# Local attention, layer norm and a routed feed-forward layer on one core: GpSimd splits a tile's attention ahead of the row's norm

## The reference

```python
qkv = x @ W_attn + b_attn                      # 16 heads of 16
scores = einsum(q, k) * scale                  # causal, 64 rows back
out = softmax(scores) @ v
x = layernorm(x + out @ W_proj + b_proj)       # eps 1e-5
# routed feed-forward: argmax of 8 router logits picks the expert
inter = gelu(x @ W1[e] + b1[e])                # 256 -> 1024
y = inter @ Wo + bo + x
y = (y - mean(y)) * rsqrt(var(y) + 1e-12) * gamma + beta
x = layernorm(y)
```

## Time and profile before

| | |
|---|---|
| time, median of 3 runs | 637.53 us (636.71 to 638.04) |
| time of the profiled execution | 635.29 us |
| its span | 633.6 us |
| granted TensorE clock, mean | 0.916 of full |
| PE busy | 83% of the span |
| DVE, ACT, POOL busy | 63%, 58%, 51% |

### The profile page before, as it was taken

How to read it: one execution, slowest core, us unless ns; L and a number is a source line. 1 busy time by engine, 2 the same in 40 slices (tenths; PEclk the granted TensorE clock), 3 DMA queues, 4 the chain that set the end, 5 groups by cost and what they waited for, 6 DMA issues and landing times. The chain is left out here.

```text
span 633.6 us, 24795 instructions
## 1 busy us (share of the span) xinstructions
PE 523.3 (83%) x8587; PEld 456.2 (72%) x8587; DVE 397.6 (63%) x1071; ACT 370.0 (58%) x832; POOL 325.9 (51%) x568
## 2 busy tenths in 40 slices
PE   4698878788878878788787761799999999999990
PEld 3487667677766767667675660699999999999880
DVE  3445546575565657565674446578888888887533
ACT  4357466675656566667564632476667666765450
POOL 8612333533442353344533433168888888887333
PEclk9779799996998999999995765799999999999996
DMA  9787597465645655665464200223322222222000
GB/s 207 166 219 209 154 228 197 127 176 129 178 134 136 186 149 157 152 178 175 134 156 137 64 12 24 68 62 101 96 87 78 77 78 70 77 66 66 24 16 6
DMA packets 94888, 75.34 MB, mean 119 GB/s; under 512 B 37030, under 2 KB 88367, under 8 KB 94770
## 3 DMA queue, kind: packets, MB, share of 16 engines
q1 hardware_dynamic: 91410, 65.31, 39.8%
q0 software_dynamic: 3264, 8.41, 3.8%
q10 hardware_dynamic: 96, 0.04, 0.0%
HBM read 43.63 MB, written 23.62 MB: 106 GB/s over the span
## 5 line engine op out<-in xcount | busy, mean ns | idle before, releaser
L1409 PE MATMUL ps<-v_even,w_hi 128*128 128x128 f16 (+1 forms) x1280 | 170.3, 215 | 1.9 <-issue 0.8
L1409 PE MATMUL ps<-v_even,w_lo 128*128 128x128 f16 (+1 forms) x640 | 132.0, 214 | 0.2
L835 ACT ACTIVATE probs<-ps,b1T 128x128 f32<-128x128 f32 (+1 forms) x320 | 87.3, 361 | 72.2 <-PE ps L1409 63.7
L1391 PE MATMUL ps<-wo_hi,ks 128*128 128x256 f16 x576 | 128.6, 272 | 1.0 <-DVE ks L1084 1.0
L1409 PEld LDWEIGHTS ps<-v_even,w_hi 128*128 x1280 | 120.7, 98 | 7.0 <-issue 3.6
L868 DVE TENSOR_REDUCE mx<-ps 128x4 bf16<-128x512 f32 x128 | 83.1, 685 | 22.2 <-PE ps L1190 21.2
L1391 PE MATMUL ps<-wo_lo,ks 128*128 128x256 f16 x288 | 78.5, 272 | 0.0
L1239 PE MATMUL ps<-v_odd,probs 128*64 128x17 f32 x1024 | 74.0, 215 | 2.2 <-issue 2.2
L655 POOL TENSOR_TENSOR less_mean<-zero,meanvar 128x1 f32<-128x1 f32 x32 | 13.1, 408 | 119.0 <-DVE meanvar L935 118.9
L1239 PE MATMUL ps<-v_even,probs 128*64 128x17 f32 x1024 | 73.8, 215 | 0.0
L1239 PEld LDWEIGHTS ps<-v_even,probs 128*64 128x64 f32 x1024 | 69.5, 146 | 5.1 <-issue 4.5
(11 more groups left out here) (222 smaller groups left out, 1361.8 us busy)
## 6 DMA issues: line engine op xcount, KB each, us to landing
qk_s<-qk_hi SPq DMA_DIRECT2D x64, 128.0 KB
w_in<-in_L_ffn_W_dram SPq DMA_DIRECT2D x32, 256.0 KB, 3.5
v_odd<-slots SPq DMA_DIRECT2D x64, 128.0 KB, 2.1
qs<-qk_s SPq DMA_DIRECT2D x16, 384.0 KB, 4.4
ks<-qk_s SPq DMA_DIRECT2D x16, 384.0 KB, 5.2
ks<-qk_s SPq DMA_DIRECT2D x32, 144.0 KB, 4.0
v_even<-v_odd SPq DMA_DIRECT2D x63, 68.0 KB, 3.8
qk_s<-qk_lo SPq DMA_DIRECT2D x32, 128.0 KB
```

Of the source, the lines that this page charges most:

```text
L835: last = nc.scalar.activation(g[1 - p][:, ic, n * width:(n + 1) * width], ps_h[1 - p][:, half, col + n * width:col + (n + 1) * width], ACT ...
L1391: ins = mm(ps_y[p], h[p][hs][:, ic, :], wo[ws][:, ic, :], start=n == 0, stop=n == 3 * IC - 1)
L1409: up_ins = mm(ps_h[1 - p][:, half, col + m * width:col + (m + 1) * width], weights(ws, owners[m], k, ic), sT[1 - p][ss][:, k, at], start=k ...
```

## The change

On POOL, the two operations of the split (tile it - 1) now stand ahead of the four operations of the norm (tile it - 2) in each iteration. No operation and no wait is added or taken away, and no other engine's program changes.

```diff
@@ -648,6 +648,14 @@
                     nc.gpsimd.tensor_tensor(row[n % 2][:, C:ROW], row[n % 2][:, C:ROW], two_tiles[:, :], ALU.add)\
                         .then_inc(number_done, 1)
+                n = it - 1
+                if a_tile(n):
+                    pool.wait_ge(att_done, n + 1)
+                    wait(pool, attT_done, n)
+                    nc.gpsimd.tensor_copy(att_part[0][:, :], att[:, :]).then_inc(ah_done, 1)
+                    pool.wait_ge(ah_done, n + 1)
+                    nc.gpsimd.tensor_tensor(att_part[1][:, :], att[:, :], att_part[0][:, :], ALU.subtract)\
+                        .then_inc(al_done, 1)
                 n = it - 2
                 if a_tile(n):
                     pool.wait_ge(mv_done, n + 1)
@@ -660,14 +668,6 @@
                     nc.gpsimd.tensor_tensor(shift_by[:, :], less_mean[:, :], rstd[:, :], ALU.mult)\
                         .then_inc(shift_done, 1)
-                n = it - 1
-                if a_tile(n):
-                    pool.wait_ge(att_done, n + 1)
-                    wait(pool, attT_done, n)
-                    nc.gpsimd.tensor_copy(att_part[0][:, :], att[:, :]).then_inc(ah_done, 1)
-                    pool.wait_ge(ah_done, n + 1)
-                    nc.gpsimd.tensor_tensor(att_part[1][:, :], att[:, :], att_part[0][:, :], ALU.subtract)\
-                        .then_inc(al_done, 1)
```

## The result

The changed kernel took 586.55 us (median of 6 runs, 584.51 to 591.63), the kernel before beside it 637.12 us (6 runs, 634.68 to 638.73): a ratio of 0.922, 95% interval 0.917 to 0.927. The forecast was 587. The profiled execution took 584.79 us, its span is 583.1.

The account below looks back on a forecast made before the run. PE was bound by waits for POOL's att_lo; 30.6 + 5 + 13.7 = 49.3 us off 635.29 gave 586.0, as a median 588.2, and with 1 to 2 us for earlier starts 587 us. The 8 in 10 range was 574 to 604.

Parts of the forecast that it names:

- What bounds the kernel: PE's transposes wait for POOL's att_lo, 54.0 us in 28 waits, because POOL's order puts the norm first.
- rival E: Something other than att_lo releases PE's transposes, so the reorder does nothing: 637 us, chance 0.03.
- Odd iterations: the whole wait goes: Split starts 0.06 us after att and ends 0.64 us before PE is free; the 1.61 us wait goes wholly.
- Even iterations: 0.58 us are left: Split still stands behind scatter and xin, held beside L962; 7.0 us of PE's wait stay over iterations 4 to 26.
- Iterations 2 to 27: 30.6 for the waits, 5 for the clock, 1 to 2 for the earlier start: Attention phase: att_lo waits of 37.6 us less 7.0, clock gain between 0 and 10.7, transposes starting some 0.1 us earlier.
- the stalls that were counted as staying: Four mid-stream stalls of PE in iterations 3 to 27, 8.7 us, explained by no semaphore, expected to remain.
- The last five: 13.7 us: No query and key products left: 1.7 us gained in iteration 28, 12 in the four after, between 8 and 15.4.
- the chain: Last iterations' pace if PE keeps full clock: transposes to att 6.66 us plus 1.2 for the split, 7.86 us.
- The norm costs nothing moved back: POOL's norm ends 1.2 us later relative to att; ACT's row L753 keeps 2.6 us of slack for shift_by.
- rival D: Late shift_by stops ACT at L753, ahead of its value copy, and PE behind it: 645 us, chance 0.03.
- A: Keys' way through DRAM comes late for shortened iterations, each of 12 pairs pays 1.5 us: 605 us, chance 0.11.
- B: ACT or DVE holds PE right behind, so half of each gain is lost: 602 us, chance 0.09.

Follow-up runs that it names:

- the filled kernel: The kernel before, with 24 dummy products on PE ahead of its wait for att_lo, 32 in the last five iterations: 622.10 us, ratio 0.985.
- w_lo waiting: The changed kernel, with one added wait: DVE's w_lo (L962) starts only when POOL's split of the same iteration is done: 587.41 us.

## Why the prediction was right, point by point

*What bounds the kernel* is confirmed: the wait for `att_lo` went and 50.5 us of span with it (rival E is out).

*Odd iterations: the whole wait goes.* Right. In iteration 23 the split takes 1.15 us, starts 0.07 us after `att` and is over 0.97 us before PE's transposes, of which 0.36 is a stall of PE. The 0.64 us of slack that was forecast is 0.46 to 0.97 us in most odd iterations, but 0.05 us in iterations 9 and 11. Over iterations 6 to 27 the median way into an odd iteration is 8.50 us; 8.4 was forecast.

*Even iterations: 0.58 us are left, between bounds of 0.11 and 0.58.* Right in mechanism, and near in size: from iteration 6 to 24 there are ten waits, 5.0 us together, and 0.13 us in 26, against 7.0 forecast; 0.5 to 0.6 us is the typical one. The hold fell on `att_lo` in eight even iterations (1.00 to 1.06 us instead of 0.67) and on the copy, as forecast, in only three (0.89 instead of 0.40). Both halves of the explanation were taken apart: without `xin` ahead the wait is 0, without L962 beside it it is 0.12. The rule of the Trainium skill on the shared port (SBUF — State Buffer, section "SBUF: two separate sides") was weighed in the forecast against this step; the 1.06 and 0.67 us of `att_lo` with and without L962 beside it agree with it. The way into an even iteration is 9.17 us; 9.0 was forecast.

*Iterations 2 to 27: 30.6 for the waits, 5 for the clock, 1 to 2 for the earlier start.* Together 37, measured 39.3: the waits for `att_lo` gave 32.6, and PE's busy time, where the clock shows, 6.1 (5.7 us was the whole gain of these iterations in the filled kernel). One thing that was put at nothing was not: the stalls that were counted as staying, 8.7 us, shrank to 3.2, and new waits for ACT (2.8) and a key load (2.1) took their place.

*The last five: 13.7 us, bounds 9.7 to 17.1 with iteration 28.* Measured 10.6. This is the term that was mis-sized. I had leaned to the clock staying up; it was 0.80 in this profile (0.91 in that of w_lo waiting), and a wait of 2.05 us in iteration 28, for which I had 0.5, was followed by its fall. I had read PE's own work in iteration 28 from a trace in which it had a 1.0 us stall of its own. With the clock kept by dummy products the stretch is 40.6 us, near the 39.3 of the chain (5 x 7.86). Of the 13.7 us, iteration 28 gave 1.1 (1.7 forecast) and the four after it 9.5 (12 forecast). The error of 3 us here and that of 2 us in the term above nearly cancel: that 587 was met to half a microsecond is in part luck, since runs of one kernel spread over 5 us and more.

*The norm costs nothing moved back.* Right; 2.3 us more cost nothing that the runs show. The slack is 3.1 to 3.7 us in most iterations (2.6 forecast). Past it the cost comes by another way than rival D had it, in the even iterations that were followed not through ACT's value copy but through POOL's own scatter, behind which the next split stands; for the rest of it the cause is open.

*Rivals A and B.* Neither decided. The loads of queries and keys that have a landing time in the profile take 4.0 to 4.3 us at a DMA share of 0.72 (4.0 to 4.4 before at 0.62); the last load of a pair, from which A was worked out, has none. The keys cost one wait of 2.1 us in iterations 2 to 27. ACT's part of B is there in small, 2.8 us, and grows to 6.4 once the even waits are gone.

## What to carry to other kernels

On an engine that serves two consumers, put first what the bounding engine waits for, and look how much slack the other has; here the order of six small operations was worth 8%. A wait of PE costs more than its length where the clock falls behind it, so a filled wait is a quick test of how much of a gain is the clock's. And when an operation can't start sooner, look at what else its engine does just ahead of it, and at what another engine does beside it.

## What the runs showed of the hardware that was not expected

Filling the waits with 24 to 32 useless 128x128 products an iteration made the kernel before 10 to 14 us faster, at a granted clock of 0.955 to 0.958 over the span (0.919 to 0.934 in six of the seven runs of the unfilled one beside it).

The hold between DVE's L962 and POOL's split works both ways, and the one that starts second pays. With L962 0.15 us ahead, `att_lo` takes 1.06 us instead of 0.67 (iteration 24 of the changed kernel, above). With the split first of all, `att_lo` is 0.06 us ahead, keeps its 0.67 us, and L962 takes 1.15 us instead of 0.68:

```profile
256.71 0.67 POOL L636 TENSOR_TENSOR att_lo<-att,att_hi 128x256 f16<-128x256 f32 x1
...
256.77 1.15 DVE L962 SCALAR_TENSOR_TENSOR w_lo<-w_in,w_hi 128x512 f16<-128x512 f32 x1
```

The second ends 0.53 us after the first in one case, 0.54 us in the other. So a split that starts in time is not slowed by L962; it slows L962, on an engine with time to spare.
